# Between convolution and dense stage: the last channel's store and the first x1 loads in time halves, first mixing matrices and stacks issued elsewhere

## What is computed

```python
# 0: state-space convolution along time, one kernel per channel, masked by length
mask = arange(1024) < length[b]
x = x + mask * (causal_conv(x * mask, K[channel]) + D[channel] * x * mask)
# 1: channels mixed by one of 16 matrices (64 x 64)
x = x + einsum('bct,bcd->bdt', x, weights[cond])
# 2: dense layer over time (1024 x 1024) with bias, and one of 32 adapters of rank 16
x = x + x @ base_weight.T + base_bias + (x @ A[a].T) @ Bw[a].T
# 3: dense layer over time (1024 x 1024), and one of 5 adapters of rank 32
x = x + x @ W.T + 0.5 * (x @ lora_A[l]) @ lora_B.T
```

## Time and profile before

| | |
|---|---|
| median of 3 runs | 1503.09 us (1501.48 to 1505.19) |
| span of the profiled execution, first to last instruction | 1500.9 us |
| TensorE matmul busy | 1456.2 us, 97% |
| VectorE busy | 1114.5 us, 74% |
| ScalarE busy | 631.1 us, 42% |
| POOL busy | 117.3 us, 8% |
| mean granted TensorE clock | 0.995 |
| DMA | 276.16 MB, 184 GB/s over the span |

### The profile page before, as it was taken

The page is one execution under the profiler, slowest core; times in us unless marked ns, Lnnn a source line. Parts: engine busy times, 40 slices in busy tenths (PEclk is TensorE's granted clock), DMA queues, the critical chain, the costliest instruction groups (busy, mean ns, idle before and its releaser), DMA issues.

```text
span 1500.9 us, 33974 instructions
## 1 busy us (share of the span) xinstructions
PE 1456.2 (97%) x10624; PEld 1404.1 (94%) x10624; DVE 1114.5 (74%) x2330; ACT 631.1 (42%) x1249; POOL 117.3 (8%) x188
## 2 busy tenths in 40 slices
PE   6989989999999997999999999999999999999998
PEld 5877879999999997999999999999999999999998
DVE  7975388888888885777777777777777777777674
ACT  4331256665656562343343343343343343334332
POOL 3451210000000000000000000000000000000000
PEclk9999999999999998999999999999999999999999
DMA  8133168888888877456556556556556656645652
GB/s 306 33 134 99 42 220 277 274 277 273 274 272 274 273 242 228 128 158 198 146 157 196 145 163 191 145 160 195 142 151 193 160 147 179 177 147 166 191 147 78
DMA packets 121380, 276.16 MB, mean 184 GB/s; under 512 B 23897, under 2 KB 64349, under 8 KB 118689
## 3 DMA queue, kind: packets, MB, share of 16 engines
q1 hardware_dynamic: 111308, 241.28, 54.1%
q10 hardware_dynamic: 10038, 34.46, 5.8%
HBM read 200.72 MB, written 74.95 MB: 184 GB/s over the span
## 4 chain that ended last, share of the span: by engine, by line
PE 87%; DVE 6%; DMA 3%; POOL 1%; issue 1%; ACT 1%; SPq 0%; DVEq 0%; ACTq 0%; POOLq 0%
PE ps L1602 23%; PE ps L1603 23%; PE ps L1234 13%; PE ps L1573 8%; PE ps L1245 6%; PE ps L1136 4%; PE ps L1225 3%; PE ps L1610 2%; PE ps L1612 2%; PE ps L1237 2%; DMA out<-y_out 1%; PE ps L1584 1%; DVE p L810 1%; DVE b3t L906 1%; DMA b_d<-b_last 1%
## 5 line engine op out<-in xcount | busy, mean ns | idle before, releaser
L1602 PE MATMUL ps<-weights,xs 128*128 128x256 f32 x1536 | 397.4, 289 | 0.0
L1603 PE MATMUL ps<-weights,xs 128*128 128x256 f32 (+1 forms) x1536 | 388.8, 292 | 0.0
L1602 PE MATMUL ps<-weights,xa 128*128 128x352 f32 (+1 forms) x1152 | 329.2, 313 | 4.6 <-ACT y_out L1386 1.3
L1603 PE MATMUL ps<-weights,xa 128*128 128x256 f32 (+1 forms) x1152 | 322.7, 295 | 0.0
L1602 PEld LDWEIGHTS ps<-weights,xs 128*128 128x128 f32 x1536 | 292.5, 190 | 0.0
L1603 PEld LDWEIGHTS ps<-weights,xs 128*128 128x128 f32 x1536 | 292.4, 190 | 0.0
L1602 PEld LDWEIGHTS ps<-weights,xa 128*128 128x128 f32 x1152 | 217.0, 188 | 10.7 <-issue 10.7
L1234 PE MATMUL ps<-toep,ut 128*128 128x512 f32 (+2 forms) x1152 | 226.7, 342 | 0.0
L1603 PEld LDWEIGHTS ps<-weights,xa 128*128 128x128 f32 x1152 | 217.2, 189 | 0.0
L1234 PEld LDWEIGHTS ps<-toep,ut 128*128 128x128 f32 x1152 | 194.3, 189 | 16.6
L1362 ACT ACTIVATE a<-ps 128x512 f32<-128x512 f32 x128 | 76.5, 598 | 274.2 <-PE ps L1573 259.5
(11 more groups left out here) (223 smaller groups left out, 2182.3 us busy)
## 6 DMA issues: line engine op xcount, KB each, us to landing
lags<-kern_d SPq DMA_DIRECT2D x64, 512.0 KB, 5.2
xt<-in_xt SPq DMA_DIRECT2D x64, 512.0 KB, 6.0
x_d<-yo SPq DMA_DIRECT2D x64, 512.0 KB, 3.2
x_nat<-in_x SPq DMA_DIRECT2D x64, 512.0 KB, 3.9
x_in<-x_d SPq DMA_DIRECT2D x64, 512.0 KB, 5.6
out<-y_out ACTq DMA_DIRECT2D x63, 512.0 KB, 5.8
tab<-a_d SPq DMA_DIRECT2D x128, 128.0 KB, 2.1
stack<-b_d SPq DMA_DIRECT2D x126, 128.0 KB, 4.1
```

Source lines behind the costliest of these rows:

```text
L1602: mm(left[0], x_part, left[1], start=first and is_wide, stop=end, skip_group_check=True)
L1603: ins = mm(right[0], x_part, right[1], start=first and is_wide and H_AT[m] > 0, stop=end, skip_group_check=True)
```

## The change

- The last channel's store is split in time halves. SP issues the first half once `y_front` has counted 64, and the second after the first x1 loads.
- The x1 loads of tiles 0 and 1 are split as well. The front halves are issued in the first block, once all stores but the last back half have landed; the back halves are issued in the second block, v = 1 first, once that back half has landed. They stand ahead of SP's reads of ids.
- VectorE waits for the front halves and the back halves by semaphores of their own (`first_rows`, `x1_landed`).
- POOL clears and gathers the first mixing matrices at the end of the first block, once the last Toeplitz operand is made. In the second block it begins with a wait for the back store, ahead of `c_gath`.
- ScalarE issues the stack transfers of pair 0 after the four quarters, not before them.

```diff
--- before.py
+++ after.py
@@ -402,7 +402,16 @@
         return ap.rearrange("p (k c) -> p k c", k=2)
 
     first_rows = [sem(f"first_rows{v}") for v in range(2)]
-    masked = sem("masked")
+    masked, x1_front = sem("masked"), sem("x1_front")
+
+    def gather(pool, n, v):
+
+        for b in range(2):
+            s = pool.value_load(index[0:1, bass.ds(4 * n + 2 * v + b, 1)], min_val=0, max_val=S1 - 1)
+            rows = slice(b * C, (b + 1) * C)
+            ins = nc.gpsimd.tensor_copy(m_gath[v][rows, b * C:(b + 1) * C], mix[rows, bass.ds(s, 1), :].squeeze(1))
+        ins.then_inc(gathered[v], 1)
+        pool.wait_ge(gathered[v], n + 1)
 
     def load_stack(eng, v, a):
 
@@ -543,11 +552,16 @@
             for v in range(2):
                 sp.dma_start(x_nat[v][:], x_rows[v]).then_inc(x_landed[v], 16)
             channel(GROUPS - 1, UNROLL - 2, loads=False)
-            channel(GROUPS - 1, UNROLL - 1, loads=False)
-            for u in range(2):
-                sp.wait_ge(x1_stored[u], count_in(GROUPS, 0, 2))
+            sp.wait_ge(y_front, C)
+            sp.dma_start(x1_d[:, C - 1, 0:HB], yo[1][:, 0:HB]).then_inc(x1_front, 16)
+            sp.wait_ge(conv_done, C - 1)
+            sp.wait_ge(x1_stored[0], count_in(GROUPS, 0, 2))
+            sp.wait_ge(x1_stored[1], count_in(GROUPS, 0, 2) - 16)
+            sp.wait_ge(x1_front, 16)
             for v in range(2):
-                sp.dma_start(x1_in[v][:], x1_rows[v]).then_inc(x1_landed[v], 16)
+                sp.dma_start(x1_in[v][:, 0:HB], x1_rows[v][:, 0:HB]).then_inc(first_rows[v], 16)
+            sp.wait_ge(y_back, C)
+            sp.dma_start(x1_d[:, C - 1, HB:T], yo[1][:, HB:T]).then_inc(x1_stored[1], 16)
 
         @block.gpsimd
         def _(pool):
@@ -637,6 +651,13 @@
             for half in range(2):
                 rows = slice(C * half, C * half + C)
                 link(tt(mix[rows], mix[rows], ident[rows, C * half:C * half + C].unsqueeze(1).to_broadcast([C, S1, C]), ALU.add))
+            pool.wait_ge(toep_lo, C)
+            pool.wait_ge(in_later, 16 * LATER)
+            for v in range(2):
+                nc.gpsimd.memset(m_gath[v][:], 0.0).then_inc(gfixed, 1)
+            pool.wait_ge(gfixed, 2)
+            gather(pool, 0, 0)
+            gather(pool, 0, 1)
 
         @block.scalar
         def _(act):
@@ -1279,6 +1300,9 @@
                     sp.dma_start(c_gath[v][rows, H3], c_adapters[bass.ds(a[b], 1), :, cols].squeeze(0)).then_inc(c_landed[v], 16)
                     sp.dma_start(c_gath[v][KS + b:KS + b + 1, H3], c_d[AR:AR + 1, cols]).then_inc(c_landed[v], 16)
 
+            sp.wait_ge(x1_stored[1], count_in(GROUPS, 0, 2))
+            for v in (1, 0):
+                sp.dma_start(x1_in[v][:, HB:T], x1_rows[v][:, HB:T]).then_inc(x1_landed[v], 16)
             a, l = [ids(sp, 0, v, B) for v in range(2)], [ids(sp, 0, v, 2 * B) for v in range(2)]
             for v in range(2):
                 for to, of in ((stack[v][H3], b3_d), (stack[v][KS + R2:KS + R2 + R3, 0], b3_d[:, 0]), (stack[v][KS:KS + 2, 1], row_d)):
@@ -1322,21 +1346,7 @@
 
         @block.gpsimd
         def _(pool):
-            for v in range(2):
-                nc.gpsimd.memset(m_gath[v][:], 0.0).then_inc(gfixed, 1)
-            pool.wait_ge(gfixed, 2)
-
-            def gather(n, v):
-
-                for b in range(2):
-                    s = pool.value_load(index[0:1, bass.ds(4 * n + 2 * v + b, 1)], min_val=0, max_val=S1 - 1)
-                    rows = slice(b * C, (b + 1) * C)
-                    ins = nc.gpsimd.tensor_copy(m_gath[v][rows, b * C:(b + 1) * C], mix[rows, bass.ds(s, 1), :].squeeze(1))
-                ins.then_inc(gathered[v], 1)
-                pool.wait_ge(gathered[v], n + 1)
-
-            gather(0, 0)
-            gather(0, 1)
+            pool.wait_ge(x1_stored[1], count_in(GROUPS, 0, 2))
             for v in range(2):
                 nc.gpsimd.tensor_copy(c_gath[v][:], ident[:]).then_inc(gfixed, 1)
             pool.wait_ge(gfixed, 4)
@@ -1348,7 +1358,7 @@
                 if not last_one:
                     pool.wait_ge(mixed, 4 * n + 4)
                     for v in range(2):
-                        gather(n + 1, v)
+                        gather(pool, n + 1, v)
 
             over_pairs(pool, pair)
 
@@ -1368,13 +1378,13 @@
                 act.wait_ge(s1_raw, n + 1)
                 copy(xs1[:, 0], s1[:], ACT.Copy).then_inc(s1_hi, 1)
 
-            for v in range(2):
-                load_stack(act, v, ids(act, 0, v, B))
             take(0, 0, a11, xa11, FIRST_BANKS[0])
             take(0, 1, a21, None, FIRST_BANKS[1])
             take(0, 2, a22, xa22, FIRST_BANKS[2])
             s1_high(0)
             take(0, 3, a12, xa12, FIRST_BANKS[3])
+            for v in range(2):
+                load_stack(act, v, ids(act, 0, v, B))
 
             def pair(n, last_one):
                 act.wait_ge(s_raw, 3 * n + 1)
@@ -1448,7 +1458,7 @@
 
             def choose_first(v, half):
 
-                dve.wait_ge(x1_landed[v], 16)
+                dve.wait_ge((first_rows, x1_landed)[half][v], 16)
                 dve.wait_ge(x_landed[v], 16)
                 dve.wait_ge(masked, 8)
                 cols = slice(half * HB, (half + 1) * HB)
```

## The result

The changed kernel takes 1509.98 us (median of 4 runs, 1508.26 to 1510.64), the kernel before 1502.96 in the same comparison: a ratio of 1.0042, 95% interval 1.0027 to 1.0056, so 6.3 us slower (4.1 to 8.4). The ratio is worked out from the single runs; the two medians lie 7.0 us apart. The forecast was 1506.3, 3.2 us slower, in a range up to 1510.0.

A forecast was written before the change was run, and what follows sets the result against it. TensorE is busy 97%, so its standstills at the seam (8.9 + 1.1 us, some 2.3 us of slow clock) bound it. SP's queue adds 3.15 us, M2's 0.6 included; 1503.09 becomes 1506.3 us, 80% range 1502.4 to 1510.0.

The forecast's parts named there:

- the likeliest case: Whole time: a difference within 0.3% (4.5 us) of the kernel before, chance 0.70.
- rival (d): SP's queue: back store lands at 579.5, x1 of pair 1 takes 7.2 us; 5 us later, time 1508; chance 0.12.
- The front halves: Seam after the convolution: front loads go out 0.65 us earlier, first mixing matmul starts 1.4 us earlier (1.0 to 2.1).
- Rival (e): Seam: front loads start no earlier than 575.3, everything 0.6 later, 1506.9; chance 0.55 together with the forecast.
- The back halves: Third quarter, first to need a back half: the chain of sums to M2 starts 1.6 us earlier (0.5 to 2.5).
- The stacks behind the quarters: ScalarE before M2: eight issues, 4.9 us, delay the copies; M2 starts 0.6 us later (-0.6 to +1.8).
- SP's own queue: SP's second block: x1 of pair 1 issued 3.15 us later, takes 6.4; first transpose 3.15 us later, waiting 2.6.
- rival (c): TensorE at M2: clock falls after a 3.3 us wait, costing up to 2.3 us; 1506.3 to 1508.6; chance 0.12.
- The edits at nothing: POOL: the early gather hides beneath the last convolution, and c_gath, after the back store, is ready before SP's use; no cost.

The follow-up runs named there:

- run 4: Kernel before, with only ScalarE's stack transfers moved behind the four quarters: 1.0032, 4.8 us over the kernel before.
- run 1: Changed kernel, with ScalarE's eight stack transfers issued before the quarters again: 1.0019, 2.9 us over the kernel before.
- run 5: Changed kernel, with SP issuing x_nat and x1 of pair 1 ahead of the adapters' rows: 1.0054, 8.1 us over the kernel before.
- run 2: Changed kernel, with SP reading its eight ids before it waits for the back store: 1.0023, 3.5 us over the kernel before.
- run 10: Kernel before, with only the first mixing matrices cleared and gathered at the end of the first block: 1.0004.
- run 12: Kernel before, x_nat and x1 of pair 1 ahead of adapters' rows, tile 1's stacks late, VectorE's H memsets ahead of its first choice: 1501.42 us, 0.9984.
- run 6: Kernel before, stack issues behind the quarters, each transfer reading one row in place of 16: 1.0007, 1.1 us over the kernel before.
- run 7: Kernel before, with the gather and the halved x1 loads all in the first block, last store whole: 1.0001.
- run 11: Changed kernel, x_nat behind channel 62's store, x_nat and x1 of pair 1 ahead of adapters' rows, tile 1's stacks after pair 0's result copies: 0.9998.
- run 9: Changed kernel, with x_nat of tiles 0 and 1 loaded behind channel 62's store: 1.0036, 5.4 us over the kernel before.

## Why the prediction was half right

Direction and order of the waits came as forecast. The size was twice as large, and the likeliest case, within 0.3%, was not the one that came. The measured median lies 0.02 us inside the end of the range; that it lies inside is luck. What came is the forecast with rival (d), SP later still (0.12), pushed beyond its ends, and on top of it a fall of the clock that no step had. By its own steps:

- **The front halves**: forecast 1.4 us sooner, measured 0.2. Two terms were mis-sized. Channel 62's store took 8.6 us, not 7.8, and the half behind it landed 6.7 after its issue, later against the y add than the whole store had (4.7 to 4.4). And the half loads took 3.1 and 3.4 us, not 2.8. Rival (e), that the front loads start no sooner, is what happened.
- **The back halves**: the back store took 3.6 us, the upper end of its bound, not 3.0; the third quarter ended at 587.1, 14.5 after the y add, 0.3 later than before, where 1.6 sooner was forecast. The loads of the back halves were quicker than thought (2.5 us).
- **The stacks behind the quarters**: forecast 0.6 us later at M2, measured 1.5; in the changed kernel this is hidden by the wait for x1. The quarters made it 1.9 worse than taken, and 1.0 came back, mostly since the first ids were read beneath the last copies (0.5 us between the start of that copy and the first issue, not 1.2). The issues cost the 4.9 us that they were given, less 0.1. The wait was 2.36 us and not 3.3.
- **SP's own queue**: forecast 3.15 us later, measured 4.3 for the issue and 7.5 us, not 6.4, for the transfer. The issue of the back store came 1.0 later against the y add than taken and the store took 0.6 longer; the queue behind it was 0.5 shorter. With both in place of the forecast's, its 3.15 becomes 5.35 at the first transpose, where 5.34 was measured. The chain from its landing to the transpose took 3.7 us, as taken over from the earlier trace rows. The wait at the transpose, forecast 2.6, was 2.14.
- **The clock** was rival (c) (0.12), with a fall at M2 after a wait of 3.3 us. It did fall there, after 2.36 us, and that cost nothing, as M4 still reached the transpose early. The 1.6 us are from a second fall, behind the transpose, which the prediction didn't name.
- **The cause.** The prediction held SP's place to be last and gave the stacks' bytes half a microsecond of x1's 6.4. That was the wrong step. Stacks late with SP on time cost 4.8 us (run 4), SP late with stacks early 2.9 (run 1), both together 6.3 and not 7.7, though the intervals don't tell these two apart. Both make the same transfer late. Run 5, which mends the cause that was held to be last, wins nothing; run 2, which mends half of it, gets x1 down 1.1 us sooner. That a late x1 meets fewer of the stacks is how I read it; the durations of the table fit. How the bytes slow x1 is open: their rows, and the tables that catch a late x1, were not tried apart.
- **The edits at nothing.** The gather was at nothing (run 10). POOL's wait for the back store was not run alone, but in the changed kernel `c_gath` is ready at 583 and SP first issues to it at 589.70.

## What to carry to other kernels

A transfer that is moved off a crowded queue is still on the same engines: ask which critical transfer it now lies beside. Here 0.75 MB in transfers of 16 rows cost the transfer beside them far more than their bytes. Where two causes make the same transfer late, mending one alone may win nothing, as run 5 did; here the place of the stacks, which share the DMA engines with it, mattered more (run 1). While a load must wait for a store, look for setup work of the consumer's engine to put there: in run 12 the memsets went under that wait and M2 came 1.9 us sooner, while splitting store and load won nothing that could be told.

## What the runs showed of the hardware

- With eight transfers of 16 rows each, 0.75 MB in all, beside it, a 512 KB load took 11.1 and 14.0 us (runs 4 and 5), and 5.4 where they moved a sixteenth of the bytes (run 6). The rate of the DMA engines was 234 GB/s against 407 at the same busy share; ahead of the tables it was 266 in run 4 against 369 in run 6.
- In the changed kernel, behind the last y add, 256 KB took 2.5 to 3.4 us to load and 3.6 to store; 512 KB took 3.57, and 4.4 in run 7.
- The clock fell after waits of 2.36 and 2.14 us in the changed kernel, 2.31 in run 11, 2.00 in run 2 and 1.83 in run 6. It stayed at full speed over waits of 2.39, 2.65 and 2.67 us before M2 in runs 5, 4 and 9, and over 2.76; in runs 5, 4 and 9 it fell only with the longer wait that followed (6.47, 3.69 and 3.68 us). So in these rows the length of the last wait alone doesn't tell whether it falls.
- ScalarE's eight issues with their ids in between took 4.8 to 4.9 us before and behind the quarters, and nearly as long with a sixteenth of the bytes (590.97 to 595.61 in run 6).
